# Statistics of layer 2's and layer 3's rows behind the copies of the turned weights in VectorE's order

## The reference, cut to what matters

```python
def _layernorm(x, g, b):
    mu = jnp.mean(x, axis=-1, keepdims=True)
    var = jnp.mean((x - mu) ** 2, axis=-1, keepdims=True)
    return (x - mu) * jax.lax.rsqrt(var + 1e-05) * g + b
...
# end of layer 2, start of layer 3
x = q + jax.nn.gelu(ctx @ Wo + bo, approximate=False)
xn = _layernorm(x, g1, beta1)                # for layer 3's queries
# behind layer 3's attention
x = residual + _mha(xn, base_n, W_qkv, b_qkv, W_o, b_o)
xn = _layernorm(x, g2, beta2)
U = (xn @ W_in.T + b_in) @ Bmat              # input of the recurrence
s = jax.nn.silu(s @ A.T) + u_t               # 512 steps, all 4 sequences
```

## Time and profile before

| | us |
|---|---|
| median of 3 runs (1512.52 to 1514.62) | 1514.4 |
| the profiled execution's own time | 1517.49 |
| its span, first to last instruction | 1515.9 |
| TensorE busy, share of the span | 1346.9, 89% |
| VectorE busy | 1039.8, 69% |
| ScalarE busy | 1065.2, 70% |
| GpSimd busy | 82.9, 5% |
| mean granted TensorE clock | 0.961 |
| loop of the 160 turns | 342.8 to about 1415 |
| last 128 steps of the recurrence alone | 1429 to 1515 |

### The profile page before, as it was taken

The page is one execution under the profiler, slowest core; times in us unless marked ns, Lnnn a source line. Parts: engine busy times, 40 slices in busy tenths (PEclk is TensorE's granted clock), DMA queues, the critical chain, the costliest instruction groups (busy, mean ns, idle before and its releaser), DMA issues.

```text
span 1515.9 us, 35932 instructions
## 1 busy us (share of the span) xinstructions
PE 1346.9 (89%) x13436; PEld 1002.6 (66%) x13436; DVE 1039.8 (69%) x2323; ACT 1065.2 (70%) x3212; POOL 82.9 (5%) x145
## 2 busy tenths in 40 slices
PE   7999899988998889999888999988899999788855
PEld 6788666665675556777666677766676777566644
DVE  4676757756787778687777777877776787777400
ACT  4556677757788887777787677777866777787422
POOL 2000111110000000000000000000000000000000
PEclk9999999999999999999999999999999999999855
DMA  8222310012221122121101211201121121110100
GB/s 296 85 87 98 103 56 2 1 46 95 58 85 42 44 75 68 42 71 57 57 30 57 83 31 58 85 29 54 47 70 43 43 85 57 29 50 9 43 0 14
DMA packets 69883, 90.42 MB, mean 60 GB/s; under 512 B 5520, under 2 KB 58896, under 8 KB 69328
## 3 DMA queue, kind: packets, MB, share of 16 engines
q1 hardware_dynamic: 69600, 87.87, 18.2%
q0 software_dynamic: 112, 0.26, 0.1%
HBM read 71.33 MB, written 16.78 MB: 58 GB/s over the span
## 4 chain that ended last, share of the span: by engine, by line
PE 60%; DVE 14%; ACT 14%; issue 10%; POOL 0%; DMA 0%; ACTq 0%; DVEq 0%; SPq 0%; POOLq 0%
PE ps L1320 14%; PE ps L1694 11%; PE ps L1327 8%; PE ps L1334 7%; PE ps L1723 6%; ACT arena L790 5%; DVE arena L1269 5%; PE ps L1768 3%; PE ps L1397 2%; PE ps L1521 2%; PE ps L1538 2%; PE ps L1677 2%; DVE arena L949 2%; ACT R L850 1%; DVE nmax L1252 1%
## 5 line engine op out<-in xcount | busy, mean ns | idle before, releaser
L1320 PE MATMUL ps<-W,arena 128*128 128x128 f32 x2896 | 434.6, 284 | 22.3 <-ACT arena L790 19.8
L1320 PEld LDWEIGHTS ps<-W,arena 128*128 128x128 f32 x2896 | 324.9, 145 | 171.5 <-issue 129.5
L790 ACT ACTIVATE arena<-ps,nmax 128x512 f32<-128x512 f32 x640 | 435.1, 686 | 0.2
L797 ACT COPY arena<-ps 128x512 f32<-128x512 f32 x320 | 187.3, 585 | 213.0 <-PE ps L1320 208.9
L1249 DVE TENSOR_REDUCE nmax<-ps 128x1 f32<-128x512 f32 x320 | 206.1, 686 | 119.5 <-PE ps L1694 83.3
L1269 DVE COPY arena<-ps 128x512 f32<-128x512 f32 x320 | 213.8, 686 | 23.7 <-PE ps L1320 13.5
L1694 PE MATMUL ps<-W,arena 32*128 32x512 f32 x1280 | 185.2, 646 | 35.3 <-DVE arena L1269 34.2
L1723 PE MATMUL ps<-arena 128*32 128x128 f32 x5120 | 173.4, 276 | 31.6 <-ACT arena L797 31.4
L1252 DVE TENSOR_REDUCE nmax<-ps 128x2 f32<-128x1024 f32 x160 | 193.7, 1210 | 0.0
L1723 PEld LDWEIGHTS ps<-arena 128*32 128x32 f32 x5120 | 130.4, 110 | 69.5 <-ACT arena L797 59.1
L790 ACT ACTIVATION_READ_ACCUMULATOR arena<-ps,nmax 128x1 f32 x640 | 131.1, 205 | 0.0
(11 more groups left out here) (240 smaller groups left out, 1648.0 us busy)
## 6 DMA issues: line engine op xcount, KB each, us to landing
W<-keys SPq DMA_DIRECT2D x48, 512.0 KB, 3.7
arena<-values SPq DMA_DIRECT2D x48, 512.0 KB, 5.1
keys<-W SPq DMA_DIRECT2D x16, 448.0 KB, 3.0
values<-W SPq DMA_DIRECT2D x16, 448.0 KB, 3.6
W<-keys SPq DMA_DIRECT2D x16, 256.0 KB, 2.8
arena<-values SPq DMA_DIRECT2D x16, 256.0 KB, 3.3
W<-in_pack SPq DMA_DIRECT2D x1, 3180.0 KB, 10.5
CX<-in_ctx SPq DMA_DIRECT2D x4, 512.0 KB, 11.0
```

The lines of the kernel that those rows point to most:

```text
L790: nc.scalar.activation(Pr[:, a, :], ps[:, a, :], ACT.Exp, bias=nmax[:, u % 32:u % 32 + 1], accum_out=den[:, u % 32:u % 32 + 1]).then_inc(s ...
L797: nc.scalar.copy(PT[:, (4 * Q + a) % 8, :, :].rearrange("p k n -> p (k n)"), psT).then_inc(sem("u_ev_act"), 1)
L1320: ins = nc.tensor.transpose(dst[:, k * P:(k + 1) * P], src[:, k * P:(k + 1) * P], ident)
```

## The change

Two numbers and one name in the tables of half-steps. Layer 2's sum of the row keeps half-step 5, under a name of its own, `row`. Its statistics go from 5 to 6, with GpSimd's root behind them; the normalised row goes from 6 to 7, and tp, xT, q and qT, which are counted from tp, go from 6, 7, 7, 8 to 7, 8, 8, 9 on their engines. Layer 3's statistics go from 3 to 4, where the normalised row and tp stay.

```diff
     step.update({0: dict(tp=3), 1: dict(f_tp=3, f_xT=4, f_h=4, bias=5, f_relu=5, f_o=5, stats=6, nrm=7, tp=7),
-                 2: dict(gelu=4, stats=5, nrm=6, tp=6), 3: dict(bias=2, stats=3, nrm=4, tp=4)}[li])
+                 2: dict(gelu=4, row=5, stats=6, nrm=7, tp=7), 3: dict(bias=2, stats=4, nrm=4, tp=4)}[li])
     tp = step["tp"]
     step.update(xT=tp + 1, q=tp + 1, qT=tp + 2, u_hT=tp + 2, u_u=tp + 2, u_out=tp + 3)
...
                 if li == 2:
                     nc.vector.tensor_tensor(orows[i], X[:, D:2 * D], w("bo2"), ALU.add).then_inc(sem("L2_pre"), 1)
-                    yield step["stats"]
+                    yield step["row"]
                     dve.wait_ge(sem("L2_gelu"), n)
                     add_more(row, row, nrm[i])
                     yield from queries("L3", n, i, row, step)
```

## The result

The changed kernel takes 1503.6 us (median of 7 runs, 1500.8 to 1513.0) against 1513.8 for the kernel before (7 runs); the ratio is 0.9942 [0.9926, 0.9959].

The account below looks back on a forecast made before the run. The loop passing from engine to engine was taken as the bound, no engine at its limit. A -9.1, B -1.5 and C's rows (+5.0, +0.8, +0.55, +0.25, +1.8) gave -2.2 us: 1512.2 us, range 1505 to 1518.

Parts of the forecast that it names:

- A: Layer 2's statistics leave the odd half-step: 0.76 us gained per row, twelve rows, 9.1 us; 0 in pass 0.
- B: Layer 2's row goes on one half-step later: 0 in passes 1 to 3, -1.5 us in pass 0.
- C: Layer 3's statistics go in front of the maxima, GpSimd's root no longer covered; front grows by up to 1.1 us.
- C first rows: Turns 74 to 76, layer 2's fourth row with layer 3's first: +0.9 us each, +0.8 in pass 0.
- C second rows: Turns 77 and 78: -0.16 us in passes 1 and 2, +0.2 in pass 3, +0.65 in pass 0.
- C third rows: Turn 79, end of the scan: -0.6 us twice, +0.65 in pass 0, +0.8 in pass 3's tail.
- C fourth rows: Turn 81 and its like: nothing gained, front's 0.7 us paid; +0.6 three times, the last one 0.
- the root wait is hidden: Faster rival: all layer 3 turns have slack for the root as turn 78, 1505.2 us; 0.37 shared with clock relief.
- root wait paid 16 times: Slower rival: VectorE stands at L885 for GpSimd, 1.1 us paid each time, 1523 us; 0.18 shared with a worse clock.
- clock relief: Rival: A's shorter TensorE idleness removes the 4.6 us lost at the lower clock, 1507.6 us; 0.37 shared with hidden root.

Follow-up runs that it names:

- l2_late: Kernel before with layer 2's delay alone: sum and statistics stay in step 5, normalisation and turn go to step 7; 1514.7 us in one run.
- u_root_twice: Changed kernel with GpSimd's root of layer 3's u rows computed twice, one behind the other; 1517.4 us.
- u_no_root: Changed kernel with the root, and so the wait for GpSimd, left out of layer 3's u rows; 1501.2 us.
- tail3: Changed kernel, but the last two layer 3 rows keep their statistics in step 3; 1502.1 and 1503.8 us, ratios 0.9915 and 0.9918.
- scan_busy_32: tail3 with one small TensorE product of 32 columns behind each closing scan step but the last; 1533.8 us.

## Why the prediction missed

The mechanism of layer 2 was right, and the sum was lost in layer 3. By the prediction's own terms, against full-clock turns:

| term | forecast | measured |
|---|---|---|
| A in nine rows (turns 62, 66, 70 and their like) | -6.8 | -6.8 |
| B, passes 1 to 3 | 0 | -1.0 |
| B, pass 0 | -1.5 | -1.7 |
| C first rows with turn 74, passes 1 to 3 | +2.7 | +1.05 |
| the same in pass 0 | +0.8 | +0.3 |
| C second rows | +0.55 | -1.65 |
| C third rows and tail | +0.25 | -0.5 |
| C fourth rows | +1.8 | +0.15 |
| sum | -2.2 | -10.1 |

C was forecast at +6.1 in all and came to -0.65, which is 6.75 of the 7.9 us that the sum missed.

- **A** held to 0.01 us: 0.755 to 0.765 us a row where the row says 0.76, nothing in pass 0, and l2_late shows that the place of the statistics is all of it.
- **B** held for turns 63 and 64 (-0.04) and for pass 0. It missed turns 71 and 72, 0.25 us shorter in each pass, which the one pair of layer 1 turns did not stand for.
- **C, second rows: the failed step.** I let turn 78's exponentials begin 0.24 us later because the maxima did. The kernel before shows that they did not follow the maxima: the first one ran straight behind ScalarE's copy of turned weights, which waited 1.46 us for TensorE and now comes as much earlier as the copies do. I had the 0.40 us that ScalarE idles for the values and set the later maxima against it. But in front of those exponentials lay a second slack, which I never read: the first maximum was through at 845.92 + 0.69 = 846.61, its exponential began at 847.03, 0.42 us later. The two together are 0.82 us. The maxima began 0.56 us before ScalarE's copy of turned weights and now begin 0.26 behind it (844.00 against 843.74), 0.82 later. One root wait just fits, and a second is paid, as u_root_twice shows. Pass 3 (-0.32) and pass 0 (+0.20) came lower than forecast too, but there u_no_root shows 0.44 and 0.16 of the root wait paid; what takes up their slack stays open.
- **C, third rows.** The loop's 0.74 a pass came instead of 0.6, for the same reason, and pass 0's +0.65 was +0.04. The tail's +0.8 was right in mechanism and came to +1.0.
- **C, fourth rows.** "Nothing is gained, and the front's 0.7 is paid" was half right. Turn 81 grew by 0.73, and turn 82, which I left out of the account, shrank by 0.68: a front that delays its own turn's maxima starts the count of the next turn late, and the end of that turn did not move. Counting a pair of turns would have shown it.
- **C, first rows.** Turn 76 at 7.46 is as forecast (7.5), turn 75 at 7.29 less than 7.6. Turn 74 lost 0.18 of its gain where I took 0.33.
- **The rival "the root wait is hidden"** named the mechanism and was given too little. Its time, 1505.2, still lay 1.6 over the result, since it only dropped costs and allowed no gain in turn 78. Against it I had set that 1.1 us more in front puts VectorE behind the scores. That is true (L885 idles 0.67 us, the maxima no longer wait) and decides nothing: what matters is who waits for the maxima, 3.2 us in the whole run, and whether that engine has other slack behind its wait.
- **The rival "root wait paid 16 times"** falls with u_no_root. Of the 14 waits in the loop, those in front of turn 76's maxima and their like in passes 1 to 3 are paid in full, those in front of turns 36, 38 and 158 in part, and eight not at all; of the two in the tail the first is paid, and the last was there before.
- **The clock** did not make the difference between the two kernels (4.1 and 4.7 us over their sums), so "clock relief" falls as an explanation. Layer 3's part did take the stretches of turns 119 and 120 away (1.6 us a profile). The clock also hid some 4 us of layer 2's part in one session and none in another, and it set the length of the changed kernel's profiled execution.

## What to carry to other kernels

When a wait is to be moved in front of an operation, ask not whether that operation would now be late, but who consumes it, and whether that consumer's other inputs come later still; read both the idle time behind the consumer and the gap in front of it, and count over the pair of turns. A free wait holds for the turns it was measured in and for as much as the slack holds: the second root wait was paid, so was the same wait in layer 2, and in six of layer 3's own 14 fronts, and in the tail, the first one was paid in full or in part. Where a loop repeats, the sum of its turns at the full clock parts effects of 0.1 us that medians with several microseconds of clock noise cannot.

## What was not expected of the hardware

One program lost none of its loop to stretches at 1.2 GHz in one profile and 4.2 us in the next (tail3; the kernel before lost 8.0 in its one), though TensorE is busy 89% of the span. Their place changes the price: 1.4 to 2.4 us for 6.8 that begin in a gelu turn, about 3 us for 6.8 behind turn 159, and 8.3 us for the 20.5 there. In the closing scan of scan_busy_32 TensorE was busy 40.00 us of 40.00 at a granted clock of 0.50. The Trainium skill ("TensorE: Matmul & The Clock Gate", section "Part 1: The HAM clock gate") has activity release the lower clock; this trace shows that a TensorE which the profile calls fully busy may stay at it all the same.
